# The last expert's second layer by row blocks, and who waits for the last stores

## The reference

```python
x = x + xattn(layernorm(x), ctx, ctx, ...)   # 16 heads of 64, then a norm with gamma, beta
x = x + attn(layernorm(x), ...)              # 16 heads of 32, rotary positions
x = x + ffn(layernorm(x), ...)
# ffn: 8 experts, each 512 -> 2048 -> 512, two of them used per token
logits = xf @ Wr + br
thresh = top_k(logits, 2)[0][:, 1:2]
weights = softmax(where(logits >= thresh, logits, -inf))
h = gelu(einsum('td,edh->eth', xf, W1) + b1)
expert_out = einsum('eth,ehd->etd', h, W2) + b2
out = einsum('etd,te->td', expert_out, weights)
```

## Time and profile before

| | |
|---|---|
| median of 3 runs | 1752.58 us (1750.35 to 1754.89) |
| profiled execution, its own time | 1766.07 us |
| its span | 1764.2 us |
| PE busy | 1677.1 us, 95% |
| DVE busy | 880.1 us, 50% |
| ACT busy | 697.0 us, 40% |
| POOL busy | 306.3 us, 17% |
| mean granted TensorE clock | 0.977 |

### The profile page before, as it was taken

One profiled execution on the slowest core, in us unless ns is written; L12 is line 12 of the kernel. 1 busy time (PEld: TensorE's weight loads), 2 busy tenths in 40 slices (PEclk: granted clock), 3 DMA queues, 4 the chain that ended last, 5 costly groups with the idle time before them and its releaser, 6 DMA issues.

```text
span 1764.2 us, 27021 instructions
## 1 busy us (share of the span) xinstructions
PE 1677.1 (95%) x10906; PEld 1410.4 (80%) x10906; DVE 880.1 (50%) x1592; ACT 697.0 (40%) x1314; POOL 306.3 (17%) x257
## 2 busy tenths in 40 slices
PE   7999999999999999999999978994999999999996
PEld 6888888888888888888888766773888888888985
DVE  4334443444444434444344566774768447548841
ACT  5333333333333333333333334443556345336631
POOL 3200211011101111011100341555211011001101
PEclk9999999999999999999999989995899999999998
DMA  6601820111101110111002630114656437427611
GB/s 223 221 5 52 134 68 20 39 55 55 50 8 52 55 52 7 52 55 52 7 7 91 221 112 28 57 41 140 233 140 209 138 94 230 145 88 237 219 34 21
DMA packets 54067, 165.10 MB, mean 94 GB/s; under 512 B 10581, under 2 KB 10965, under 8 KB 53377
## 3 DMA queue, kind: packets, MB, share of 16 engines
q1 hardware_dynamic: 38032, 131.88, 21.7%
q0 software_dynamic: 15888, 31.19, 8.5%
HBM read 143.54 MB, written 55.64 MB: 113 GB/s over the span
## 4 chain that ended last, share of the span: by engine, by line
PE 87%; ACT 3%; DVE 3%; DMA 3%; issue 2%; POOL 1%; another core or an unknown queue 0%; SPq 0%; ACTq 0%; POOLq 0%; DVEq 0%
PE psum L404 64%; PE psum L745 13%; PE psum L409 5%; PE psum L524 4%; ACT P L1331 2%; DMA out_x<-xg,meta 1%; PE psum L606 1%; DMA ya<-residuals 1%; POOL out_x L1567 0%; PE psum L678 0%; DMA xg<-expert_rows 0%; DMA raw<-in_Wv 0%; DMA xs<-in_x 0%; DVE mx L982 0%
## 5 line engine op out<-in xcount | busy, mean ns | idle before, releaser
L404 PE MATMUL psum<-ctx,Wk 128*128 128x512 f32 x1536 | 384.9, 399 | 0.0
L404 PE MATMUL psum<-Wv,ctx 128*128 128x512 f32 x1536 | 368.7, 389 | 0.0
L404 PEld LDWEIGHTS psum<-Wv,ctx 128*128 128x128 f32 x1536 | 288.3, 188 | 59.9
L404 PEld LDWEIGHTS psum<-ctx,Wk 128*128 128x128 f32 x1536 | 279.2, 188 | 55.6
L881 DVE SCALAR_TENSOR_TENSOR kT<-psum,bkc,kT 128x512 fp32r<-128x512 f32 x128 | 96.0, 750 | 387.7 <-ACT kT L1245 387.7
L404 PE MATMUL psum<-xgT,Wh 128*128 128x256 f32 (+2 forms) x1536 | 268.8, 327 | 4.9 <-issue 4.8
L404 PEld LDWEIGHTS psum<-xgT,Wh 128*128 128x128 f32 x1536 | 239.2, 191 | 26.4 <-issue 7.2
L745 PE MATMUL psum<-Wh,hs 128*128 128x512 f32 x1056 | 258.8, 391 | 0.0
L745 PEld LDWEIGHTS psum<-Wh,hs 128*128 128x128 f32 x1056 | 194.6, 188 | 36.9
L1245 ACT ACTIVATE kT<-psum,bkc 128x512 fp32r<-128x512 f32 x128 | 88.3, 690 | 248.3 <-PE psum L404 248.2
L1410 ACT ACTIVATE gl<-psum,b1c 128x512 f32<-128x512 f32 x128 | 88.0, 688 | 225.6 <-PE psum L404 225.6
(11 more groups left out here) (146 smaller groups left out, 1780.7 us busy)
## 6 DMA issues: line engine op xcount, KB each, us to landing
raw<-in_W SPq DMA_DIRECT2D x128, 512.0 KB, 4.2
expert_rows<-in_spare_rows SPq DMA_DIRECT2D x16, 1042.0 KB, 8.0
raw<-in_ctxT SPq DMA_DIRECT2D x32, 512.0 KB
xg<-expert_rows POOLq DMA_DIRECT2D x32, 256.0 KB, 5.5
low_parts<-Olo POOLq DMA_DIRECT2D x32, 128.0 KB, 2.4
oT<-low_parts SPq DMA_DIRECT2D x8, 512.0 KB, 4.9
out_x<-x SPq DMA_DIRECT2D x12, 256.0 KB
xs<-in_x SPq DMA_DIRECT2D x4, 512.0 KB, 7.2
```

The source lines that it names most:

```text
L404: mm = pe.matmul(dst, l, r, start=n == 0, stop=n == len(pairs) - 1)
```

## The change

In the last expert's job TensorE takes the last LAG tiles (13, 14 and 15) by row blocks: for each block all three tiles, nine matmuls, then a signal `y_ready`. Tile 12 stays in its place. The last block's signal counts for the blocks that this width doesn't have, so that `y_ready` always ends four higher. TensorE then waits for `y_ready` and adds the last `y_psum` itself. VectorE waits for each block's own count of `y_ready` in this job.

GpSimd's job of the last expert first fills up the count of `out_wide` with one-row transfers between two DRAM rows that nobody uses any more, for each block that this width lacks (one for MIDDLE), and returns after the last scatter is issued. SyncE waits at the end of its program for `out_added` and `out_wide` of the last expert. The waits that GpSimd leaves out come back in the second round, ahead of its first use.

```diff
@@ sync_program, at its end
+            sp.wait_ge(out_added, 32 * E)
+            sp.wait_ge(out_wide[E - 1], 32)
@@ tensor_program
+            def last_downs(q, width):
+                chunks = width // P
+                for c in range(chunks):
+                    for i in range(NI - LAG, NI):
+                        n = NI * q + i
+                        hr = hs[n % HS]
+                        if c == 0:
+                            pe.wait_ge(h_lo, n + 1)
+                        for m, (x, y) in enumerate(((0, 0), (0, 1), (1, 0))):
+                            mm = pe.matmul(bank[3 + c], hr[x][:, c * P:(c + 1) * P], Wh[i][y][:, 512:1024],
+                                           start=False, stop=i == NI - 1 and m == 2)
+                        if i == NI - 1:
+                            mm.then_inc(y_ready, 1 if c < chunks - 1 else CH - c)
+                        elif c == chunks - 1:
+                            mm.then_inc(y_psum, 1)
+                pe.wait_ge(y_ready, E - 1 + CH)
+                pe.sem_inc(y_psum, 1)
             def job(q, width, more):
                 for i in range(NI + LAG):
                     if i < NI:
                         up(q, i, width)
-                    if i >= LAG:
+                    if q == E - 1 and i == NI:
+                        last_downs(q, width)
+                    if i >= LAG and (i < NI or q != E - 1):
                         down(q, i - LAG, width)
@@ vector_program, weighted(q)
-                    if c == 0:
-                        v.wait_ge(y_ready, q + 1)
+                    if q == E - 1:
+                        v.wait_ge(y_ready, q + c + 1)
+                    elif c == 0:
+                        v.wait_ge(y_ready, q + 1 if q < E else q + CH)
                     else:
                         v.wait_ge(y_psum, NI * (q + 1))
@@ gpsimd_program, job(q, width, more)
                 g.wait_ge(meta_in[q % 2], 16 * (q // 2 + 1))
+                if q == E - 1:
+                    for c in range(width // P, CH):
+                        g.dma_start(residuals[0, c:c + 1], residuals[1, c:c + 1]).then_inc(out_wide[q], 16)
                 for c in range(width // P):
                     g.wait_ge(y_done, CH * q + c + 1)
                     g.indirect_dma_start(out, ...)
+                if q == E - 1:
+                    return
                 g.wait_ge(out_added, 32 * (q + 1))
@@ gpsimd_program, second round
             with g.If(rows_of[E] > WIDE):
+                g.wait_ge(out_added, 32 * E)
+                g.wait_ge(out_wide[E - 1], 32)
+                g.wait_ge(y_done, CH * E)
+                g.sem_inc(scattered, 1)
                 fetch_rows(E)
```

## The result

The changed kernel takes 1745.85 us (median of 20 runs, 1742.24 to 1751.41), the kernel before 1752.07 (median of 20). The ratio is 0.9961, 95% interval 0.9951 to 0.9971: 6.8 us faster by the ratio, 6.2 by the medians. Forecast was 7.0.

The account below looks back on a forecast made before the run. TensorE's queue plus what runs after its last matmul was taken to bound the kernel. Gains of 2.65 us (order) and about 4.3 us (GpSimd not waiting) sum to 7.0: 1752.58 - 7.0 = 1745.6 us, range 1743.0 to 1751.0.

Parts of the forecast that it names:

- the two parts: Kernel's end: new order of the last matmuls, 2.65 us; GpSimd no longer waiting for the landing, about 4.3 us.
- Order of the matmuls: Last 27 matmuls: block 0 complete 2.74 us earlier, no stall on tile 15; last scatter 2.65 us earlier.
- rival (e): TensorE stalls on tile 15, so block 0 comes no earlier; gain 4.4 us, time 1748.2; chance 0.02.
- Landing: Last scatter starts at 1748.5 and lands 5.6 us later, at 1754.1.
- GpSimd's DRAIN: Program's end: starts 0.3 us after the last issue at 1750.06, takes 6.56 us, covers the landing; end 1757.2.
- rival (c): GpSimd's closing branch stalls 4.75 us in the open before its DRAIN; gain 2.6 us, time 1750.0; chance 0.05.
- Rival (a): GpSimd's DRAIN begins its 6.56 us only after the last landing; gain 3.3 us, time 1749.3; chance 0.17.
- Rival (b): GpSimd's long DRAIN belongs to the profiled execution alone; gain some 3.0 us, time 1749.6; chance 0.10.
- Rival (d): GpSimd's DRAIN pays 6.56 us per scatter in the air, 19.7 us; 5.8 us slower, time 1758.4; chance 0.03.
- TensorE's end: TensorE's closing branch of 4752 ns from 1747.3 ends at 1752.1, DRAIN at 1752.2, 5 us before the end.
- Sum: Whole kernel: span end from 1764.2 to 1757.2, 7.0 us less: 2.65 from the order, about 4.3 from GpSimd's wait.

Follow-up runs that it names:

- e2: Kernel before, with only SyncE waiting in GpSimd's place and the one-row transfer added, TensorE's order unchanged; ratio 0.9976.
- e6: Kernel before, with one more GpSimd DRAIN at the start of the last expert's job; ratio 0.9965.
- e5: Changed kernel with an early GpSimd DRAIN in the last job and TensorE's wait moved into the second round; 1744.15 us, ratio 0.9956.
- e4: Changed kernel with one more GpSimd DRAIN behind the one-row transfer at the start of the last job; ratio 0.9965.
- e9: Changed kernel with early GpSimd DRAIN and TensorE's wait moved, but GpSimd waiting for the landings and SyncE not; 1744.11 us, ratio 0.9954.
- e1: Kernel before, with only the new order of the last 27 matmuls and its signals, GpSimd still waiting for the landings; ratio 0.9983.
- e7: Kernel before, with 64 more one-row GpSimd transfers at the start of the last expert's job; one run, tail 20.81 us.
- r2: Changed kernel with early GpSimd DRAIN and TensorE's wait moved, run again; 1743.39 us, ratio 0.9941 to the kernel before.
- r1: Changed kernel run once more without further edits; 1747.37 us, ratio 0.9965 to the kernel before.
- e3: Changed kernel with TensorE's wait for y_ready and its y_psum increment moved into the second round; ratio 0.9961.

## Why the prediction was right, step by step

The forecast (faster, 1745.6) met 1745.85. The direction and the two parts were right; that the number fits so well is in part luck, as the steps show.

- **Order of the matmuls.** Right: no stall on tile 15, and 27 matmuls in 6.28 us; block 0, 1 and 2 start at -4.04, -2.00 and +0.04 us from the last matmul, where the sum had -4.06, -2.01 and +0.04; rival (e), a stall, has nothing for it. The last scatter was put 1.27 us behind it and starts at 1.06, outside the bounds of the term (2.86 us earlier than before, where 2.74 was the upper end). What I missed is that a wait taken up by the one-row transfer changes how the scatter waits.
- **Landing.** 7.01 us behind the last matmul; 1754.1 - 1747.23 = 6.9 was forecast. Two misses cancel here: the last scatter starts 0.2 us earlier and takes 5.95 us to land, not 5.6.
- **GpSimd's DRAIN.** Half right. As forecast, it begins ahead of the landing and part of its 6.56 us is hidden there. But the sum let it run by its own clock, 0.3 + 6.56 from the end of the last issue, and put the landing well inside it; its end came 2.8 us behind the landing in the sum only because of the numbers taken. The runs tie its end to the landing instead: it follows it by 3.59 us, in four executions whose landings lie 3.6 to 4.4 us behind the end of the last issue. The term was 0.9 us too small and would have missed by more with a longer flight. Which part of the DRAIN's work has to wait for the landing, no run shows. It started earlier than I put it, 1.40 us behind the last matmul, since GpSimd's queue passed its branches at 1736.5 and 1736.65 with the last scatter not begun: rival (c), a branch of GpSimd that stalls in the open, falls with these rows of 0.04 us. The early start did not help, for the landing sets the end.
- **Rival (a)**, all of it behind the landing, is refuted by e2 and by the changed kernel; but 3.6 of the 6.56 us do stand there. **Rival (b)**, a short DRAIN in timed runs, is refuted by e6, a DRAIN more and 0.35% less time. (Its gain adds up to 3.3 us and not to the 3.0 given; both are far from the 6.2 to 6.8 measured.) **Rival (d)**, the DRAIN's whole time for each flying scatter, 19.7 us in all, is refuted by DRAINs of 8.7 to 10.1 us.
- **TensorE's end.** Wrong, without harm. I gave its queue one closing branch, ending at 5.0 us behind the last matmul, and it has two; the new wait put both behind the last matmul, and its DRAIN came at 10.2. The row of the first branch (3288 ns at 1743.0) lay in the same trace. Had GpSimd's DRAIN been as short as in e5, this step would have cost the change 2 to 3 us (e4). The rule of the Trainium skill, "Runtime: NRT & Kernel Launch", Instruction fetch mechanics, is that a taken branch to a page not held stalls for a fetch. TensorE's rows of 3.3 to 5.9 us agree with it, though none names a fetch; GpSimd's branches, to which I applied it in rival (c), show no such stall.
- **Sum.** Tail forecast 9.97, measured 10.85; gain forecast 7.0, measured 6.1 in the tail and 6.2 to 6.8 in the times. The DRAIN's term was 0.9 us short, 0.1 of it from the landing and 0.8 from the DRAIN's end behind the landing (3.59 and not 2.8), and nothing else of size stood against it.

The other rule weighed (the Trainium skill, "VectorE: DVE Perf Modes", The DRAIN you can't avoid) is that the DRAINs of pre- and postamble take a constant 12 ns or so on all five engines. At the program's start these traces come near it for four engines, with 7 to 10 ns, and not for GpSimd, with 167 to 169. At the end they don't agree: 57 to 66 ns for VectorE and TensorE, 235 to 547 for ScalarE, 7 or some 50 for SyncE, and GpSimd's 377 to 10245 hold the backlog. That these last DRAINs are the ones the page means is not shown.

## What to carry to other kernels

Read the rows of the program's end too: 7 of the 17 us behind the last matmul were one DRAIN that no busy count shows. Where GpSimd has issued many transfers, put a DRAIN into a stretch in which it idles; here one instruction gave 0.35% (0.18 to 0.51), as much as the whole change. When two changes at one end don't add up, count each run from its landing as well as from its last matmul: that parts what moved the landing from what follows it. And a wait added at the end of an engine's queue costs what is queued behind it, closing branches included: put it into the rare path that needs it.

## What the runs showed of the hardware

GpSimd's DRAIN grows with the number of transfers that GpSimd has issued since its last DRAIN, though all of them have landed: 0.17 us with none (the program's start), 0.38 with three (e6 and e9), 6.24 with 166 (e6 and e9), 6.56 with 169 (before and e1), 10.24 with 233 (e7). With transfers in the air it goes on until they have landed: it ends 0.15 us behind the landing where nothing else is left to do (e4, e5, r2), and 3.59 us behind it where the backlog of 167 earlier transfers is left (changed, r1, e2, e3), though it had begun 5.1 to 6.5 us ahead of the landing. So less than half of the backlog's 6 us was hidden, and why just this much was not tried.
